# Time mixing stage: exponentials of the running state first, and the numerator of the gated sum on GpSimd

## The reference, cut to what matters

```
xk, xv, xr = three mixes of the normalised input with itself, shifted by one token
k = xk @ Wk.T;  v = xv @ Wv.T;  r = sigmoid(xr @ Wr.T)
w = -exp(time_decay)
for every token t:                      # per sequence and channel; aa = bb = 0, pp = -1e38 at first
    p   = max(pp, u + k[t]);  e1 = exp(pp - p);  e2 = exp(u + k[t] - p)
    y[t] = (e1*aa + e2*v[t]) / (e1*bb + e2)
    p2  = max(pp + w, k[t]);  e1b = exp(pp + w - p2);  e2b = exp(k[t] - p2)
    aa, bb, pp = e1b*aa + e2b*v[t], e1b*bb + e2b, p2
x = x + (r * y) @ Wo.T
```

## Time and profile before

| | us |
|---|---|
| median of 3 runs (lowest to highest) | 1659.83 (1659.17 to 1660.93) |
| the profiled execution | 1660.14 |
| its span from first to last instruction | 1658.4 |
| busy in the span: PE, DVE, ACT, POOL | 1524.2, 1018.2, 673.7, 342.9 |
| mean granted TensorE clock | 0.962 of full speed |

### The profile page before, as it was taken

One profiled execution on the slowest core, in us unless ns is written; L12 is line 12 of the kernel. 1 busy time (PEld: TensorE's weight loads), 2 busy tenths in 40 slices (PEclk: granted clock), 3 DMA queues, 4 the chain that ended last, 5 costly groups with the idle time before them and its releaser, 6 DMA issues. The chain is left out here.

```text
span 1658.4 us, 20886 instructions
## 1 busy us (share of the span) xinstructions
PE 1524.2 (92%) x7643; PEld 1075.6 (65%) x7643; DVE 1018.2 (61%) x1911; ACT 673.7 (41%) x1300; POOL 342.9 (21%) x250
## 2 busy tenths in 40 slices
PE   7999999999999748998996899899889999989998
PEld 5788888877767524576885355455674555556887
DVE  6777777721423789346445789899446777744444
ACT  1355555510221230301312699896341555543221
POOL 3100000001301300104005069497561000000000
PEclk9999999999899979989998989899899999999999
DMA  6200000051421300013651013131001333101222
GB/s 188 73 14 19 13 19 13 7 127 31 138 88 60 133 1 0 1 51 132 214 181 57 27 64 102 51 100 66 17 1 27 84 95 91 22 1 52 59 58 64
DMA packets 93906, 105.26 MB, mean 63 GB/s; under 512 B 13909, under 2 KB 77513, under 8 KB 93694
## 3 DMA queue, kind: packets, MB, share of 16 engines
q1 hardware_dynamic: 90750, 95.86, 19.4%
q0 software_dynamic: 3072, 8.30, 1.6%
HBM read 83.39 MB, written 14.55 MB: 59 GB/s over the span
## 5 line engine op out<-in xcount | busy, mean ns | idle before, releaser
L995 POOL TENSOR_TENSOR m_state_c<-m_state,m_c 128x1024 f32<-128x1024 f32 x64 | 153.2, 2396 | 85.2 <-DVE m_state L2874 69.3
L2874 DVE TENSOR_TENSOR_SCAN m_state<-m_decay,psum 128x512 f32<-128x512 f32 x128 | 148.9, 1207 | 14.2 <-POOL m_state_c L995 9.4
L3022 DVE TENSOR_REDUCE a_max_pieces<-psum 128x4 f32<-128x512 f32 (+2 forms) x176 | 107.9, 639 | 52.0 <-PE psum L1744 30.8
L2231 ACT ACTIVATE a_probT<-psum 128x512 f32<-128x512 f32 (+1 forms) x176 | 97.3, 558 | 89.7 <-PE psum L1771 85.9
L1612 PE MATMUL psum<-m_state_c,ident 128*128 128x512 f32 x256 | 121.1, 596 | 3.8 <-POOL m_state_c L995 3.8
L938 POOL TENSOR_TENSOR rstd<-var_eps,half_neg 128x4 f32<-128x4 f32 x18 | 20.2, 1120 | 423.8 <-DVE var_eps L2317 423.8
L1093 PE MATMUL psum<-ones_bf,ident_bf 128*128 128x512 bf16 x311 | 80.7, 417 | 21.6 <-DVE xn L2331 4.9
L2162 ACT ACTIVATE m_b_inputT<-m_dtuT,m_bcT 128x256 f32<-128x256 f32 x218 | 93.1, 496 | 0.9 <-PE psum L1604 0.8
L2582 DVE TENSOR_TENSOR f_h<-f_silu,psum 128x512 f32<-128x512 f32 (+1 forms) x46 | 31.5, 686 | 99.8 <-ACT f_silu L1985 99.0
L1985 ACT ACTIVATE f_silu<-psum 128x512 f32<-128x512 f32 (+1 forms) x46 | 27.5, 597 | 158.4 <-PE psum L1276 158.4
L1604 PEld LDWEIGHTS psum<-ident,m_b_inputT 128*128 128x128 f32 x512 | 62.1, 151 | 42.7 <-DVE m_state L2874 35.2
(11 more groups left out here) (457 smaller groups left out, 3528.0 us busy)
## 6 DMA issues: line engine op xcount, KB each, us to landing
f_fc<-in_L_ffn_fc_w_dram SPq DMA_DIRECT2D x16, 1024.0 KB, 6.0
m_c<-m_c_rows SPq DMA_DIRECT2D x32, 512.0 KB, 3.7
f_share<-f_share_rows SPq DMA_DIRECT2D x32, 256.0 KB, 3.3
f_out_rows<-f_out SPq DMA_DIRECT2D x15, 256.0 KB, 2.2
f_slot_rows<-f_out SPq DMA_DIRECT2D x1, 2560.0 KB, 9.8
f_rows_in<-f_slot_rows SPq DMA_DIRECT2D x10, 256.0 KB, 3.0
wkv<-in_L_attn_Wk_dram SPq DMA_DIRECT2D x16, 128.0 KB, 2.2
wkv<-in_L_attn_Wv_dram SPq DMA_DIRECT2D x16, 128.0 KB, 2.2
```

The costliest lines, as they stand in the source:

```text
L995: pool.tensor_tensor(hc2[c][:], h2[c][:], c_wide[v][:].rearrange("p (b s) -> p b s", b=BATCH), ALU.mult).then_inc(s_hc, 1)
L2231: act.activation(probT3[n % 2][:, PROB3[i]:PROB3[i] + wide], bank[TURNED3[at % 3]][:, 0:wide], ACT.Exp).then_inc(s_exp3, 1)
L2874: ins = dve.tensor_tensor_scan(h2[c][:, b], dec2[c][:, b], bank[4 + 2 * c + b], 0.0, ALU.mult, ALU.add)
L3022: dve.tensor_reduce(max_of3[n % 2][:, int(diagonal), t_, heads[0]:heads[-1] + 1], o, AX.X, ALU.max).then_inc(s_max3, 1)
```

## The change

It touches `recurrence1` on VectorE, ScalarE and TensorE, and adds `gated_sums` on GpSimd.

- VectorE makes the arguments in the order `e2b`, `e1b`, `e1`, `e2`; `ww` and the maximum come between the pairs. It waits for only two exponentials before e2b*v, and additionally for its own four arguments, since `mx` is overwritten. The two scans for `aa` come first, then the two for `bb`. e2*v, e1*aa, the addition of the two and the product with the gate are gone from it. After the denominator is complete it adds one to `s_nmax`, takes the reciprocal, and waits for GpSimd's `s_prob` before the last product.
- ScalarE takes the first two exponentials of half 0 between the copies of k and the first copy of v, and the other two between the two copies of v.
- GpSimd computes, for each half, e2*v as soon as four exponentials are there, and, when VectorE has counted up `s_nmax`, e1*aa, the sum, and the sum times the gate.
- TensorE's `keep_busy` runs 56 matmuls in place of 80.
- `s_nmax` and `s_prob` are semaphores of the first attention, counted further here.

```diff
@@ -367,6 +367,8 @@
...
+        SUMS_1, GATED_1 = 3 * HEADS0 * BATCH, HEADS0 * BATCH
+        EXPONENTS1 = 3, 2, 0, 1
@@ -998,6 +1000,22 @@
...
 
+            def gated_sums():
+
+                for m in range(KT):
+                    V, R = (o[:, m].rearrange("p (b s) -> p b s", b=BATCH) for o in (vv, sr))
+                    e1, e2, _, _, ww, mx = (o[:] for o in tm)
+                    pool.wait_ge(s_ex, 4 * m + 4)
+                    pool.wait_ge(s_kvr, KT + m + 1)
+                    ch.step(pool.tensor_tensor(ww, e2, V, ALU.mult))
+                    pool.wait_ge(s_nmax, SUMS_1 + m + 1)
+                    ch.step(pool.tensor_tensor(mx, e1, aa[:, :, 0:SEQ], ALU.mult))
+                    ch.sync()
+                    ch.step(pool.tensor_tensor(mx, mx, ww, ALU.add))
+                    ch.sync()
+                    pool.wait_ge(s_kvr, 2 * KT + m + 1)
+                    pool.tensor_tensor(mx, mx, R, ALU.mult).then_inc(s_prob, 1)
+
             def clear_stack(i):
@@ -1062,6 +1080,8 @@
...
                     clear_v()
+                if n == 3:
+                    gated_sums()
                 if n == 4:
@@ -1427,7 +1447,7 @@
...
                         pe.wait_ge(s_ex, 8)
-                        keep_busy(6, 80)
+                        keep_busy(6, 56)
                     pe.wait_ge(s_y1, k + 1)
@@ -2057,15 +2077,18 @@
...
                 act.activation(decay[:], cols_b[:, ROWS_B["L1_attn_time_decay"][0]:][:, 0:KT], ACT.Exp).then_inc(s_decay, 1)
                 shifted(2, "L1_attn_ln1_w", "L1_attn_ln1_b")
-                def exponents(m):
-                    for c in range(4):
+                def exponents(m, first, end):
+                    for c in range(first, end):
+                        e = tm[EXPONENTS1[c]]
                         act.wait_ge(s_arg, 4 * m + c + 1)
-                        act.activation(tm[c][:], tm[c][:], ACT.Exp).then_inc(s_ex, 1)
+                        act.activation(e[:], e[:], ACT.Exp).then_inc(s_ex, 1)
 
                 for n, dst in enumerate((kk, vv, sr)):
-                    if n == 2:
-                        exponents(0)
+                    if n == 1:
+                        exponents(0, 0, 2)
                     for m in range(KT):
+                        if n == 1 and m == 1:
+                            exponents(0, 2, 4)
                         act.wait_ge(s_kvr_mm, 4 * n + 2 * m + 2)
                         o = dst[:, m].rearrange("p (b s) -> p b s", b=BATCH)
@@ -2073,7 +2096,7 @@
...
                             act.activation(o, src, ACT.Sigmoid).then_inc(s_kvr, 1)
-                exponents(1)
+                exponents(1, 0, 4)
                 shifted(3, "L1_attn_ln2_w", "L1_attn_ln2_b")
@@ -2704,35 +2727,34 @@
...
                         ch.step(dve.tensor_tensor_scan(pp[:, b, 1:], decay[:, m:m + 1].broadcast_to([P, SEQ]), K[:, b],
                                                        START, ALU.add, ALU.max))
+                    ch.sync()
+                    dve.tensor_tensor(e2b, K, pp[:, :, 1:], ALU.subtract).then_inc(s_arg, 1)
+                    dve.scalar_tensor_tensor(e1b, pp[:, :, 0:SEQ], decay[:, m:m + 1], pp[:, :, 1:], ALU.add,
+                                             ALU.subtract).then_inc(s_arg, 1)
                     ch.step(dve.tensor_scalar(ww, K, col_b("L1_attn_time_first", m), None, ALU.add))
                     ch.sync()
                     ch.step(dve.tensor_tensor(mx, ww, pp[:, :, 0:SEQ], ALU.max))
                     ch.sync()
-
                     dve.tensor_tensor(e1, pp[:, :, 0:SEQ], mx, ALU.subtract).then_inc(s_arg, 1)
                     dve.tensor_tensor(e2, ww, mx, ALU.subtract).then_inc(s_arg, 1)
-                    dve.scalar_tensor_tensor(e1b, pp[:, :, 0:SEQ], decay[:, m:m + 1], pp[:, :, 1:], ALU.add,
-                                             ALU.subtract).then_inc(s_arg, 1)
-                    dve.tensor_tensor(e2b, K, pp[:, :, 1:], ALU.subtract).then_inc(s_arg, 1)
-                    dve.wait_ge(s_ex, 4 * m + 4)
+                    dve.wait_ge(s_ex, 4 * m + 2)
                     dve.wait_ge(s_kvr, KT + m + 1)
+                    dve.wait_ge(s_arg, 4 * m + 4)
                     ch.step(dve.tensor_tensor(mx, e2b, V, ALU.mult))
                     ch.sync()
                     for b in range(BATCH):
                         ch.step(dve.tensor_tensor_scan(aa[:, b, 1:], e1b[:, b], mx[:, b], 0.0, ALU.mult, ALU.add))
+                    for b in range(BATCH):
                         ch.step(dve.tensor_tensor_scan(bb[:, b, 1:], e1b[:, b], e2b[:, b], 0.0, ALU.mult, ALU.add))
-                    ch.step(dve.tensor_tensor(ww, e2, V, ALU.mult))
                     ch.sync()
-                    ch.step(dve.tensor_tensor(mx, e1, aa[:, :, 0:SEQ], ALU.mult))
+                    dve.wait_ge(s_ex, 4 * m + 4)
                     ch.step(dve.tensor_tensor(e2b, e1, bb[:, :, 0:SEQ], ALU.mult))
                     ch.sync()
-                    ch.step(dve.tensor_tensor(mx, mx, ww, ALU.add))
-                    ch.step(dve.tensor_tensor(e2b, e2b, e2, ALU.add))
+                    dve.tensor_tensor(e2b, e2b, e2, ALU.add).then_inc(s_nmax, 1)
+                    dve.wait_ge(s_nmax, SUMS_1 + m + 1)
+                    ch.step(dve.reciprocal(e2b, e2b))
                     ch.sync()
-                    ch.step(dve.reciprocal(e2b, e2b))
-                    dve.wait_ge(s_kvr, 2 * KT + m + 1)
-                    ch.step(dve.tensor_tensor(mx, mx, R, ALU.mult))
-                    ch.sync()
+                    dve.wait_ge(s_prob, GATED_1 + m + 1)
                     dve.tensor_tensor(K, mx, e2b, ALU.mult).then_inc(s_y1, 1)
                 for c in range(4):
                     o = xn[:, 2 * c:2 * c + 2, :]
```

More of the change, by code:

```diff
@@ L177, in build @@
         s_sc = sem("a0_scores_product")
-        s_nmax = sem("a0_max_ready")
+        s_nmax = sem("a0_max_or_m1_sums_ready")
         s_exp = sem("a0_exp_done")
         s_inv = sem("a0_reciprocal_or_f1_one_hot_ready")
-        s_prob = sem("a0_prob_ready")
+        s_prob = sem("a0_prob_or_m1_gated_sum_ready")
         s_pT_mm = sem("a0_prob_turned_or_f1_last_expert_spread")
```

## The result

| | before | after |
|---|---|---|
| median, us (lowest to highest; 5 rounds side by side) | 1660.93 (1659.17 to 1664.64) | 1652.0 (1647.4 to 1652.51) |
| the profiled execution | 1660.14 | 1652.26 |
| its span | 1658.4 | 1650.5 |
| mean granted TensorE clock | 0.962 | 0.959 |

The account below looks back on a forecast made before the run. VectorE's chain in the stage was taken as the bound: 17.4 + 2.1 + 7.5 = 27.0 us per half saves 9.0, less 1.5 for TensorE's clock, net 7.5, giving a median of 1652.3 us; range 1645.8 to 1655.0.

Parts of the forecast that it names:

- The sum for the stage: Both halves, first scan to last product: 27.0 us each, from 33.51 and 29.53, together 9.0 us saved.
- Up to the reciprocal: VectorE from first scan to start of the reciprocal: 17.4 us in each half, without the wait and three instructions.
- The waits: VectorE's idle for exponentials, 5.10 us in half 0 and 1.12 in half 1, gone in both halves.
- the copy of v: ScalarE, half 0: first copy of v ends by 585.2, ready before VectorE's multiply at 587.4.
- The collision: GpSimd's e2*v beside VectorE's scans for aa: engines take turns, 2.1 us on the path in each half.
- Rival 1: Scans and GpSimd don't take turns: 24.9 us per half, 13.2 saved, clock kept, 1646.6 us; chance 22%.
- The numerator behind the denominator: GpSimd's other three instructions beside the 6.55 us reciprocal: 7.5 us with two 0.20 waits, VectorE idle about 1 us.
- Rivals 2 and 4: Second: reciprocal holds GpSimd off, 1665.4 us, 8%. Fourth: neither turns nor a visible numerator, 1644.8 us, 4%.
- Rival 3: Gain partly given back by another collision, slower GpSimd or worse-timed clock falls: 1655.3 to 1658 us; chance 8%.
- The clock: TensorE's clock falls ahead of the second output product, which takes 5.20 instead of 3.72: 1.5 us lost.
- The gap ahead of the output product: TensorE idle between filler and y of half 1: grows from 1.66 to 4.4 us, with filler taking 13.8.
- a sign that it is wrong: Prediction fails if time between stage and kernel end changes by more than 1 us.

Follow-up runs that it names:

- memset: Changed kernel with a memset of the same tile in place of GpSimd's e2*v, so the numerator lacks that term; run once, 1649.46 us.
- two products: Changed kernel with GpSimd's e2*v issued twice, the second behind a wait for the first; run once, 1662.10 us.
- the order alone: Changed kernel's new order, but whole numerator on VectorE, nothing on GpSimd, 74 filler matmuls; median 1655.59 us, ratio 0.9968 to the kernel before.
- late product: Changed kernel with GpSimd's e2*v issued only once the denominator is complete; median 1653.41 us, ratio 0.9961 to the kernel before.
- e2*v on VectorE: Changed kernel with e2*v moved back to VectorE, GpSimd keeping its other three, 61 filler matmuls; median 1649.26 us, ratio 0.9930 to the kernel before.
- 66 matmuls: Changed kernel with 66 in place of 56 filler matmuls ahead of the output product; median 1650.18 us, ratio 0.9938 to the kernel before.
- ScalarE's inverse without the second filler: Changed kernel with ScalarE making the reciprocal as exp(-ln(denominator)), numerator on VectorE, GpSimd idle, 46 filler matmuls; median 1641.99 us, ratio 0.9892 to the kernel before.

## Why the prediction was right, and where it was not

**The sum for the stage.** 27.0 per half was forecast and 26.81 and 26.82 measured: 9.41 saved, not 9.0. Term by term:

- Up to the reciprocal, 17.4: 599.61 - 579.96 is 19.65 and the collision in it is 2.06, so 17.59. The waits are gone as argued; the copy of v ends at 586.76, later than the 585.2 of the argument, but 2.4 us before it is needed. The start to start distances of before, and 0.1 for a wait on the engine's own result, were a good measure.
- The collision, 2.1: measured 2.06 by the longer scans, 2.03 by taking GpSimd out of them, 2.02 by the memset, 2.10 by a second product. The sign was settled by choosing the row with the operands of the new pair (both inputs in SBUF) and not the row with the instruction's name (the state scans, with one input in PSUM). Rival 1, which rested on the latter, falls.
- The numerator behind the denominator, 7.5: measured 606.77 - 599.61 = 7.16. Here is the mis-sized term. GpSimd's waits for its own last result are 0.07 (599.66 + 2.17 to 601.90) and 0.08 (601.90 + 2.34 to 604.32), not the 0.20 read from the earlier trace rows, a row with another form; and the three instructions took 2.17, 2.34 and 2.34, not 2.37 each. VectorE's idle was 0.60, not 1.
- Rivals 2 and 4 fall in the same rows: GpSimd starts 0.05 behind the reciprocal, not 6.55, and both costs that rival 4 denied are there. Rival 3 had a further collision and a clock that falls at worse moments; the halves show no such collision, and from the last product to the first relu the clock falls once after, as it did before.

**The clock.** The gap ahead of the output product is 3.90, where 4.4 was forecast: the exponentials take 1.1 and not 0.97, the filler starts 0.2 later for it and takes 13.95 and not 13.8, so it ends 0.3 later, and y is there 0.2 earlier. The clock falls in the gap, and the product takes 5.18 (5.2 forecast). The price of 1.46 is there, but the sum is not: the step that failed is that this price comes on top. The kernel before kept its clock in the gap of 1.66 and paid 16 us later, at the gap of 2.33 ahead of the feed-forward network, of which no row was quoted; the kernel after doesn't lose the clock there, in either of its two profiles. Why not is not shown: the fall ahead of it doesn't explain it by itself, since three other runs fell at both. So 1.27 comes back (8.60 less 7.33 of ScalarE's idle), and the stretch from last product to first relu grows by 0.19, not 1.5. I had read the windows around the stage and not those of the next stage that the clock reaches. The prediction named a change of over 1 us between the stage and the end as a sign that it is wrong. Counted from the end of the output product it changed by -1.6, so in this part it was; counted from the last product of VectorE the two clock terms cancel, and it changed by -0.2.

**What made up for it.** The first scan comes 1.67 later in the profiled run, in code that the change doesn't touch. Against it stand 1.27 given back by the clock, 0.4 more in the halves and 0.35 in everything behind: 1652.6 was forecast for this execution, and 1652.26 is hit within 0.4 because errors of opposite sign cancel. The start of the stage lay between 576.1 and 580.5 in the thirteen profiled runs of this study, and the same kernel's times spread by 5 us. A hit closer than some 2 us is luck here.

**Where the start moves.** The profile puts the idle time ahead of the first scan down to issue (1.70 before, 2.46 after, none in the run of the order alone), but in all three the scan starts 0.06 to 0.07 behind ScalarE's copy of k, and the copy waits for TensorE. Before, and then after:

```profile
571.87 8.75 PE L1393 MATMUL psum<-m_xk,m_WkT 128*128 128x512 f32 x16 [0.59 <-DVE m_xk L2680]
577.22 1.01 ACT L2073 COPY m_k<-psum 128x1024 f32<-128x1024 f32 x1 [10.73 <-PE psum L1393]
```

```profile
572.76 9.51 PE L1413 MATMUL psum<-m_xk,m_WkT 128*128 128x512 f32 x16 [0.16 <-DVE m_xk L2703]
578.88 1.01 ACT L2096 COPY m_k<-psum 128x1024 f32<-128x1024 f32 x1 [11.49 <-PE psum L1413]
```

TensorE's clock in one microsecond of this product, before and after:

```profile
576.00:577.00 1.00, 1.00 (x3) 1.00 0.00 0
```

```profile
576.00:577.00 1.00, 1.00 (x2) 0.50 0.00 0
```

From the start of the product to the copy it takes 5.35 before, 6.12 after, and 3.74 in the run of the order alone, where the clock stays at 1.00. The filler ahead of the block's transposes shows the same: its clock is back at full speed at about 561.5 before and 564 after, and the transposes start 1.52 later against VectorE's normalised tile (3.25 and 4.77 behind it). VectorE's tile itself comes 0.62 earlier after; 1.52 and 0.77 less 0.62 are the 1.67. So the first line of the table is TensorE's clock as well. Why it comes back later in one run than in another was not tried and stays open, and so does what spreads the ten runs of the order alone over 9 us.

## What to carry to other kernels

When work moves from VectorE to GpSimd, price it by the operands: here, with two inputs in SBUF on each side and GpSimd's instruction begun just before, it cost the length of that instruction less some 0.3 us on VectorE's path (2.40 and 2.06); beside the one-input reciprocal, or a scan with one input in PSUM, it was free. So place GpSimd's work beside a long one-input instruction, and if one piece doesn't fit there, leave it on VectorE, where 1.2 us was cheaper than 2.06. And before moving a long reciprocal's neighbours, ask whether another engine can make the reciprocal.

For the clock, read the windows up to the next long busy stretch, not only those of the gap that is changed: a fall that is avoided in one gap may come in the next, and some of these runs fell at both. In the traces of the change with more filler, it paid only when both gaps were closed.

## What the runs showed of the hardware that was not expected

- Turns between VectorE and GpSimd go instruction by instruction in both directions: with two products in line each scan took 3.25 and 3.30 instead of 1.2, and GpSimd's second product 3.14 instead of 2.40.
- The reciprocal, 6.55 us for 128x1024, ran undisturbed beside three GpSimd instructions with two inputs each.
- On ScalarE a logarithm and an exponential with the table load between them take 3.4 us for the same tile, about half of VectorE's reciprocal; with the load ahead of the logarithm it is 4.7.
- A gap of 2.33 to 2.34 us stands ahead of the feed-forward network in ten of the traces. In seven the clock fell in it or within 1.5 us behind it (before, late product, e2*v on VectorE, 66 matmuls, two products, memset, ScalarE's inverse without the second filler); in three it stayed at 1.00 (the change, twice, and the order alone). A gap of 2.02 lost it, and gaps of 1.65 to 1.89 did not. The length of a gap alone doesn't decide; what does was not isolated.
